# Building a count matrix in batches of eight windows instead of twelve, in four PSUM banks instead of six

## The reference

```python
edge_index = jnp.stack([src, dst])
h = jnp.maximum(_layernorm(x), 0.0)
# block 0: 12 steps of message passing
h = tanh(h @ W_in + b_in)
for _ in range(12):
    agg = segment_sum(h[src], dst, num_segments=N) / deg
    diff = tanh(gelu(agg @ W1 + b1) @ W2 + b2)
    h = h + (diff - decay * h) * 0.5
x = x + h
# block 1: two graph convolutions
h = jnp.maximum(_layernorm(x), 0.0)
h = relu(gcn_conv(h, G1, gb1)); h = gcn_conv(h, G2, gb2)
return x + h
```

## Time and profile before

| | |
|---|---|
| time, median of 3 runs | 1383.92 us (1383.03 to 1383.93) |
| time of the profiled execution | 1382.67 us |
| its span, first to last instruction | 1380.5 us |
| PE busy in the span | 1274.5 us (92%) |
| DVE busy | 402.6 us (29%) |
| ACT busy | 316.9 us (23%) |
| POOL busy | 46.4 us (3%) |
| mean granted TensorE clock | 0.976 of full |
| one-hots L959, 106 operations | 92.4 us busy |
| window matmuls L555, 625 | 55.0 us busy |
| evictions L753, 52 | 75.5 us busy |
| first matmul of the steps (L628) | at 135.38 us |

### The profile page before, as it was taken

How to read it: one execution, slowest core, us unless ns; L and a number is a source line. 1 busy time by engine, 2 the same in 40 slices (tenths; PEclk the granted TensorE clock), 3 DMA queues, 4 the chain that set the end, 5 groups by cost and what they waited for, 6 DMA issues and landing times. The chain is left out here.

```text
span 1380.5 us, 17337 instructions
## 1 busy us (share of the span) xinstructions
PE 1274.5 (92%) x7202; PEld 709.8 (51%) x7202; DVE 402.6 (29%) x792; ACT 316.9 (23%) x452; POOL 46.4 (3%) x48
## 2 busy tenths in 40 slices
PE   2875999999999999999999999999999999659898
PEld 1754455554554555645556455564555545424445
DVE  7898013022130121301312113112130221472412
ACT  1898013112131121311312113121131221300100
POOL 4900000000000000000000000000000000000000
PEclk7899999999999999999999999999999999879899
DMA  3000200000000000000000000000000000130111
GB/s 94 1 1 1 60 1 0 0 0 0 0 0 0 0 0 0 0 0 0 0 0 0 0 0 0 0 0 0 0 0 0 0 0 0 46 93 0 35 29 32
DMA packets 23673, 13.59 MB, mean 10 GB/s; under 512 B 6076, under 2 KB 23254, under 8 KB 23393
## 3 DMA queue, kind: packets, MB, share of 16 engines
q1 hardware_dynamic: 21550, 12.28, 3.3%
q10 hardware_dynamic: 1698, 0.66, 0.2%
q0 software_dynamic: 400, 0.33, 0.1%
HBM read 9.42 MB, written 3.44 MB: 9 GB/s over the span
## 5 line engine op out<-in xcount | busy, mean ns | idle before, releaser
L628 PE MATMUL ps<-adj,hi 128*128 128x512 f16 (+2 forms) x2450 | 815.3, 353 | 31.1 <-DVE lo L1153 25.7
L630 PE MATMUL ps<-adj,lo 128*128 128x512 f16 (+2 forms) x2352 | 796.9, 353 | 0.0
L628 PEld LDWEIGHTS ps<-adj,hi 128*128 128x128 f16 x2450 | 238.3, 98 | 282.1 <-issue 46.2
L630 PEld LDWEIGHTS ps<-adj,lo 128*128 128x128 f16 x2352 | 229.5, 98 | 243.5 <-issue 23.8
L1065 DVE TENSOR_TENSOR ps<-ps,bias 128x512 f32<-128x512 f32 (+1 forms) x84 | 53.7, 640 | 547.8 <-PE ps L651 547.8
L793 ACT ACTIVATE scratch<-ps 128x512 f32<-128x512 f32 (+1 forms) x84 | 46.3, 552 | 655.3 <-DVE ps L1065 655.3
L642 PE MATMUL ps<-scratch,w 128*128 128x512 f32 (+2 forms) x336 | 141.0, 542 | 15.0 <-ACT scratch L785 15.0
L785 ACT ACTIVATE scratch<-ps,b1c,cols 128x512 f32<-128x512 f32 (+2 forms) x168 | 113.4, 722 | 156.6 <-PE ps L642 155.6
L651 PEld LDWEIGHTS ps<-w,scratch 128*128 128x128 f32 x1200 | 143.3, 192 | 6.3
L651 PE MATMUL ps<-w,scratch 128*128 128x128 f32 x1200 | 146.1, 275 | 0.0
L1058 DVE TENSOR_TENSOR scratch<-ps,scratch 128x512 f32<-128x512 f32 (+2 forms) x84 | 52.0, 619 | 189.5 <-PE ps L642 132.4
(11 more groups left out here) (124 smaller groups left out, 203.4 us busy)
## 6 DMA issues: line engine op xcount, KB each, us to landing
scratch<-rdeg_scratch SPq DMA_DIRECT2D x1, 1562.5 KB
scratch<-dinv_scratch SPq DMA_DIRECT2D x1, 1562.5 KB, 7.0
state<-in_x_dram SPq DMA_DIRECT2D x5, 256.0 KB, 4.7
scratch<-in_x_dram SPq DMA_DIRECT2D x5, 256.0 KB, 3.8
x_scratch<-state SPq DMA_DIRECT2D x5, 256.0 KB
state<-x_scratch SPq DMA_DIRECT2D x5, 256.0 KB
out_dram<-state SPq DMA_DIRECT2D x5, 256.0 KB
adj<-adj SPq DMA_DIRECT2D x1, 390.6 KB, 4.0
```

The source lines that it names most:

```text
L628: nc.tensor.matmul(bank, hi[:, k, :], adj[:, k, c0:c0 + n], start=(at == 0), stop=False)
L630: mm = nc.tensor.matmul(bank, lo[:, k, :], adj[:, k, c0:c0 + n], start=False, stop=(k == K_ORDER[-1][0]))
```

## The change

Three numbers and the two places that name the banks:

```diff
@@ -55,11 +55,11 @@
 BANK_WIN = 4
-BANKS = 3
+BANKS = 2
 BATCH = BANKS * BANK_WIN
 BATCHES = WINDOWS // BATCH
 RUN = 2
-EVERY = 4
+EVERY = 6
 TURN_AT = [2 + EVERY * g for g in range(NG)]
 PROD_AT = [b + EVERY // 2 for b in TURN_AT]
 LO_AT = [b + 4 for b in PROD_AT]
@@ -560,7 +560,7 @@
                 for w in range(BATCH):
-                    mm = window(u, w, ps[:, 3 * u + w // BANK_WIN, :], w % BANK_WIN)
+                    mm = window(u, w, ps[:, BANKS * u + w // BANK_WIN, :], w % BANK_WIN)
                 mm.then_inc(s_mm[u], 1)
@@ -753,7 +753,7 @@
                 nc.scalar.activation(
                     adj[:, :, bass.ds((i * 2 + u) * BATCH * WIN, BATCH * WIN)].rearrange(
                         "p k (b c) -> p b k c", b=BANKS),
-                    ps[:, 3 * u:3 * u + 3, 0:BANK_WIN * WROW].rearrange(
+                    ps[:, BANKS * u:BANKS * u + BANKS, 0:BANK_WIN * WROW].rearrange(
                         "p b (k c) -> p b k c", k=TILES), ACT.Copy).then_inc(s_ev[u], 1)
```

## The result

The changed kernel takes 1399.68 us (median of 4 runs, 1398.72 to 1401.81) against 1383.47 us before (4 runs, 1382.52 to 1383.93). The ratio is 1.012, 95% interval 1.0103 to 1.0138: slower by 16.2 us. The forecast was 1391.6 us with a range of 1387.2 to 1395.4. The direction was right; the size (+7.7) was about half of what came (+16.2), and the time lies outside the range.

What follows compares the result with a forecast made beforehand. VectorE's one-hots were taken to set the pace of the build, with ScalarE close behind in the entry part. Terms 2.9 + 5.6 - 0.8 = +7.7 us gave 1391.6 us (+0.56%), range 1387.2 to 1395.4 us.

Steps and rivals of the forecast that it cites:

- fixed cost of small operations: VectorE's one-hots in the build: 52 more operations each pay about 0.055 us that doesn't shrink with size, +2.9 us.
- waits for TensorE at full clock: Entry part: VectorE waits 8.2 us behind entry products after the change, 2.6 before, +5.6 us.
- ends: End of the build: four matmuls fewer save 0.32 us and a smaller eviction 0.44, -0.8 us; the start 0.
- clock falls: TensorE's clock in the entry part: no term in the sum, only a rival at 4 in 100.
- The first group: First entry group: ScalarE loads a table before its first tanh, so VectorE waits 1.83 us there.
- TensorE's clock falls while it waits longer in the entry part: Rival, entry part: at half clock 2.68 us of matmuls double in six groups, +16, about 1407 us; 4 in 100.
- 2.68 us for a full group: Clock rival, entry part: the chain's 2.68 us of matmuls double at half clock in each of six groups.
- the shadow: Behind each entry product: VectorE has only two short batches to fill TensorE's 3.61 us chain, waits 1.24 us per full group.
- The rival by which only the fixed cost counts: Rival, build: the time behind each product is filled, so +2.1 us, 1386.0 us; 9 in 100.
- Full pay for small operations: Rival, one-hots: each operation pays its whole 136 ns non-streaming part, +11.2, 1395.1 us; 4 in 100.
- ScalarE as the bound: Rival, evictions: each would cost over 1.184 us; at 1.25, +5 on top, 1396.7 us; 3 in 100.
- the faster side: Rival: half-clock dip behind the build vanishes, giving back 1.7 us, no cost elsewhere, 1381.4 us; 3 in 100.

Runs made afterwards that it cites:

- the kernel with three fillers: Changed kernel plus three unused 128-column identity matmuls behind each entry batch from the fourth on that has no product: median 1391.57 us, ratio 1.0066.
- before with the low half 6 behind: Kernel before the change with the low half placed 6 batches behind its product instead of 4: median 1383.40 us, ratio 0.9998.
- 12 windows with a group every 6: Kernel before the change, still batches of 12 in six banks, but an entry group every 6 batches (72 windows instead of 48): 1395.63 us, ratio 1.0079.
- the profiles of two kernels: Changed kernel with three unused matmuls per entry batch, 1391.57 us; batches of 12, entry group every 6, four unused matmuls before each batch's window matmuls, 1386.01 us.
- one filler per batch: Changed kernel with one unused 128-column identity matmul per entry batch instead of three: median 1398.75 us, ratio 1.0115.
- three fillers when the low half was moved as well: Changed kernel with three unused matmuls per entry batch and the low half 6 batches behind its product instead of 4: 1389.17 us, ratio 1.0040.
- The last kernel above: Kernel before the change with split product, ScalarE's table loaded early, unused matmuls before each batch of 12 and 24 behind the last window: 1384.11 us, ratio 1.0002.
- the split product: Changed kernel with the bias matmul behind its batch, and tile matmuls, tanh and high half two batches later: 1399.09 us, ratio 1.0105.

## Why the prediction was wrong

Its terms, against what the runs show:

| term | predicted, us | measured, us |
|---|---|---|
| fixed cost of small operations | +2.9 | +3.5 (a batch is 1.192 us, not 1.184) |
| waits for TensorE at full clock | +5.6 | +6.3 (7.7 less 1.4) |
| ends | -0.8 | -0.7 |
| clock falls | 0 | +6.1 |

The full-clock terms give +9.1 us, where the forecast had +7.7; with the falls they make +15.2, which is what the first matmul moved. The fixed cost is from TensorE's batches 1.19 us apart in the loop, 78 x 1.192 - 52 x 1.72. The 7.7 us of waits after are those of the kernel with three fillers, 7.2 us idle in six groups and 0.09 of overlap each. The waits before are where the forecast's term was too small. It took as waiting whatever was left of 55.26 us when each batch is priced at 1.72, 2.6 us. In the trace before, VectorE's timeline has three waits there:

```profile
44.37 3.62 DVE L959 TENSOR_TENSOR scratch<-scratch 128x1536 f16<-128x1536 f16 x4 [0.17 <-PE ps L555]
48.38 3.64 DVE L959 TENSOR_TENSOR scratch<-scratch 128x1536 f16<-128x1536 f16 x4 [0.39 <-PE ps L555]
56.78 3.62 DVE L959 TENSOR_TENSOR scratch<-scratch 128x1536 f16<-128x1536 f16 x4 [0.54 <-PE ps L555]
```

They are 1.1 us, 1.4 with the overlap. The rest is batches that last longer in the entry part (eight operations took 7.23 us from 61.00 and 6.95 from 92.25), and the kernel after has that too (5.03 and 4.85). The first group waits 1.2 instead of 1.83: ScalarE had time to load its table while the product ran, so that step was over-priced.

The step that failed is the clock. "TensorE's clock falls while it waits longer in the entry part" stood among the rivals with 4 in 100, as a case of its own priced at +16 us. It came at four of seven products. The excess over 1.23 in the three full groups is 1.5, 2.0 and 2.0 us and 0.7 in the last, 6.1 together, and taking the falls away with fillers moves the first matmul by 5.8 us. The forecast had 2.68 us for a full group; it is less because the clock fell only when batch p was multiplied and the product had begun (1.00 up to 63.5 us). So the forecast's sum had a fall at nothing, and this is the larger part of the miss: 6.1 us, where all the terms at full clock together were 1.4 us too small. The 1.3 us behind the build are not settled. They are within what this stretch varies by: the same work behind the first matmul takes 1243.8 to 1246.9 us in the fourteen profiles here.

Why it got 4 in 100: I held the stretch behind the entry part against it, where TensorE is busy 19.71 of 33.20 us at full clock. Such a share over a long stretch does not tell whether the clock holds. In the changed kernel's loop it held (17.37 us busy of 28.00, clock 1.00), but in two other kernels it fell in stretches like that, without a product (before with the low half 6 behind, at 107.5 us; 12 windows with a group every 6, at 136.1). And the two errors of the change were not independent, as the forecast had them: the longer wait in the shadow stretches TensorE's work between products, and a fall at a product then lengthens the same wait.

Shown: the falls cost the changed kernel some 6 us of the build, and enough filler removed them from the profiles of two kernels (clock 1.00 from 46 to 144 us in the one, to 136 in the other), where one filler per batch did not. That idle time of TensorE has to do with the falls is what these pairs speak for. Not shown: what decides a single fall. One remained with three fillers when the low half was moved as well. The last kernel above had one in a window in which TensorE was busy 5.04 of 6 us. The kernel before with the low half 6 behind had three falls without longer waits at full clock. The groups of one kernel, alike in work, fall at one product and not at the next. Whether a fall depends on the moment at which a gap comes rather than on its length was not tested.

The rival by which only the fixed cost counts fell with the waits of 1.23 us. Full pay for small operations fell with batches of 1.192 us, and ScalarE as the bound with its idle time of 0.15 us before each eviction in the loop. Of the faster side, the half clock right behind the build did not come (1.00 from 150.6 to 162.5 us), but it came later (0.50 over 163.0 to 166.3), and the stretch behind the first matmul got no shorter. Of the Trainium skill's two figures ("VectorE: DVE Perf Modes", "The TRN2 errata") the table's 58 cycles stand nearer: an estimated 3.1 us against a measured 3.5, start to start.

## What to carry to other kernels

Before making a pipelined batch smaller, look for work of fixed size that stands between batches, add up its chain to the point where the bounding engine may go on, and count what that engine has to do in the meantime; here the low half, by where it stood, was worth seven microseconds of the median in either kernel, more than half of it through the clock. Where such a chain runs on TensorE and leaves it new idle time, price its matmuls at both clock levels and give the low level a real chance, even where another stretch of the same kernel keeps the full clock at a lower busy share. And check a wait removed for what is next late, as with the split product, whose high half was then waited for instead.

## What the runs showed of the hardware that was not expected

TensorE's granted clock can fall in the middle of a kernel, with no long wait ahead of it: TensorE's waits ahead of the changed kernel's four falls are 0.45 to 1.55 us. There it stays at 0.50 for 3.4 to 6.8 us and then comes back while the same pattern goes on. All four of its falls begin in a float32 product, but a product isn't needed: in other kernels here falls begin ahead of one or in stretches that have none. One fall at a product costs up to 2.0 us with batches of 8 and 2.8 with batches of 12. TensorE doing more, by three 128-column matmuls per batch that nobody reads, made a kernel 8 us faster (1399.68 to 1391.57 us). And the changed kernel's loop kept the clock at a lower load than its entry part (windows after):

```profile
114.00:142.00 28.00, 17.37 (x189) 12.58 (x186) 28.00 (x48) 24.33 (x25) 0.00 (x0) 1.00 0.00 0
```
